# Two reorderings in a fused graph kernel: where the vector engine masks the moved score words, and how the first aggregation group is cut into pieces

## The chip, the cores and the metric

The kernel runs on one core of a Trainium2 chip. The metric is the device time of one execution in microseconds (us). The engines are named as the profile names them: PE (TensorE), DVE (VectorE), ACT (ScalarE), POOL (GpSimd) and SP (SyncE, which here only issues DMAs).

## What is computed

4096 nodes with 128 features, and a dense 4096 x 4096 adjacency of zeros and ones. Two layers, each behind a layer norm and a relu:

```python
h = jnp.maximum(_layernorm(x, axis=-1), 0.0)
# layer 0: attention over the edges
norm2 = jnp.linalg.norm(h, axis=1, keepdims=True)
cos = beta[0] * (h @ h.T) / (norm2 @ norm2.T + 1e-07)
P = jax.nn.softmax(cos + (1.0 - adj) * -1000000000.0, axis=1)
x = x + P @ h
h = jnp.maximum(_layernorm(x, axis=-1), 0.0)
# layer 1: mean over the neighbours
deg = jnp.clip(jnp.sum(adj, axis=1, keepdims=True), 1.0)
x = x + h @ W_self + (adj @ h / deg) @ W_neigh
```

## The kernel before

The attention is cut into 72 steps, k = 0 to 71. Step k handles a pair of 128-row tiles against a group of 512 rows: `PAIR[k] = (s, p, both)`. Cosines are symmetric, so one block of scores serves the pair twice where `both` holds: once as it is (the near side) and once turned (the far side).

For each step, in two halves of 512 columns (c = 0 and 1):

- PE multiplies the scores, six products for the two halves (L1058), into a ring of three PSUM banks. `ring_free` makes each item of the ring wait until the item three places earlier has been read out for the last time; for a score half that is its `low_part`.
- ACT takes the exponential twice, once as fp16 into `word` (L600) and once in fp32 in place (L601).
- DVE subtracts the two for the fp16 remainder, `low_part(k, c)` (L834). Both halves of a number then lie in one 32-bit word of `word`.
- POOL multiplies the words by the adjacency, `mask_near(k)` (L453), and PE multiplies the result with the table of features, `attend_near(k)` (24 matmuls, L1164, L1166, L1167).
- For most far sides PE turns the words (L1069) and DVE masks them, `mask_far` (L845). For 13 steps, the `MOVED` ones, the words are turned otherwise: DVE transposes blocks of 32 (`transpose_blocks`, L855), SP stores them to memory and fetches them back in another order into `moved_words`, and about four steps later DVE masks them, `mask_moved` (L866). The step in which PE uses them is their host, and `GUEST[k + 1]` is the moved step whose host is k + 1. PE uses the far words in `attend_far` (24 matmuls, L1139, L1141, L1142). The far sums lie in one bank, and DVE adds them to the rows with `spill` (L881, L886) before PE may start the next far pair.

PE's order in step k: the scores of step k + 2, `attend_far` of the far pair of this step if it has one, some transposes and products of the second layer, the turns for the next step, `attend_near(k)`. DVE's order in its step k is written out in `attention`: `low_part(k + 2, 0)`, `spill`, `mask_far(k + 1)`, `low_part(k + 2, 1)` and around these the rest. `mask_moved(GUEST[k + 1])` stands in DVE's step k; PE uses its result in its step k + 1, right behind the scores of k + 3. All engines work in the order of their code. Adjacency tiles come by DMA: the near ones issued by POOL (`load_near`, L445), the far ones by SP into the two buffers of `stage`, and POOL (L472) or ACT (L575) converts these into one byte each.

The names `item_next` and `RING[AT["score", k + 2, 1] + 1][0]` of the change ask what stands in the ring behind the second score half of step k + 2: the next score, or a transpose (`unit`, `h2`) or a `product` of the second layer.

Behind the attention PE aggregates (L1184): 8 groups of 512 rows, 128 matmuls each. Its first group is taken in pieces, `first_group(tiles, a, b)`, as filling between the last items of the second layer's features (`h2_transposes`, L1093; `h2_products`, L1108 to L1110). These items form the list `LATE` and alternate between two banks. Between them ACT makes the relu rows (`second_h`, L608), rounds the transposes (`h2_high`, L614), and DVE takes the rest (`h2_low`, L901).

Of the kernel before, what the change touches and what calls it, by code (L numbers as in the profile page):

```python
# [5 lines left out]
def gnn_program(nc, x_in, adj_in, beta_in, w_self_in, w_neigh_in, out):  # L6
# [12 lines left out]
    NP = len(PAIR)  # L19
# [7 lines left out]
    GUEST = {HOST[k]: k for k in MOVED}  # L27
    FAR_AT = [GUEST.get(k, k if k in NORMAL else None) for k in range(NP)]
# [3 lines left out]
    RING = [("score", 0, 0), ("score", 0, 1), ("score", 1, 0), ("score", 1, 1)]  # L32
# [13 lines left out]
    AT = {item: i for i, item in enumerate(RING)}  # L46
# [24 lines left out]
    with ctx:  # L71
# [108 lines left out]
        def far_adj(k, flat):  # L180

            s, p, _ = PAIR[k]
            g = p * 2 // TPS
            at = (g * T + s * TPS) * ROWS
            block = flat[:, at:at + TPS * ROWS].rearrange("p (t c) -> p t c", c=ROWS)
            return block[:, :, (p * 2 % TPS) * P:(p * 2 % TPS + 2) * P]
# [65 lines left out]
        def ring(buffer, k, c=0, chunks=2):  # L252

            at = k % 2 * TILE + c * ROWS
            return buffer[:, at:at + chunks * ROWS]
# [9 lines left out]
        def far_sem(m):  # L265
            return s_adjt_a if m % 2 else s_adjt_p
# [407 lines left out]
        def _(dve):  # L674
# [54 lines left out]
            def unit_low(g):  # L729

                dve.wait_ge(s_uhi, g + 1)
                dve.tensor_tensor(unit_lo(g * TPS, TPS), ps[:, transpose_bank(g), :], unit_hi(g * TPS, TPS), ALU.subtract
                                  ).then_inc(s_ulo, 1)
# [68 lines left out]
            def row_stats(s):  # L802

                dve.wait_ge(s_evac, 2 * (s + 1))
                for t in range(TPS):
                    done = step_of(dve.bn_stats(stats2[:, 6 * t:6 * (t + 1)], x_row(s * TPS + t)))
                return done

            def row_moments(s, done):

                dve.wait_ge(s_step, done)
                if s >= 2:
                    dve.wait_ge(s_rs2, s - 1)
                for t in range(TPS):
                    dve.bn_aggr(mv2(s)[:, t, :], stats2[:, 6 * t:6 * (t + 1)]).then_inc(s_var2, 1)

            def scale_scores(k, c):

                p, f = PAIR[k][1], ring(word, k, c, 1)
                at = 3 * (2 * k + c)  # L820
                dve.wait_ge(s_inv, 32 * (k + 1))
                dve.wait_ge(s_scores, 2 * k + c + 1)
                dve.tensor_scalar(f, f, inv_eps[:, 2 * p + c:2 * p + c + 1], 1.0, ALU.mult, ALU.add).then_inc(s_factor, 1)
                dve.wait_ge(s_factor, at + 1)
                dve.tensor_scalar(f, f, FACTOR_MAX, None, ALU.min).then_inc(s_factor, 1)
                dve.wait_ge(s_factor, at + 2)
                dve.reciprocal(f, f).then_inc(s_factor, 1)
                dve.wait_ge(s_factor, at + 3)
                dve.tensor_tensor(score(k, c), score(k, c), f, ALU.mult).then_inc(s_scaled, 1)

            def low_part(k, c):

                dve.wait_ge(s_exp, 2 * k + c + 1)
                dve.tensor_tensor(half(word16, k, c, 0, LOW, TPS), score(k, c), half(word16, k, c, 0, HIGH, TPS), ALU.subtract  # L834
                                  ).then_inc(s_elo, 1)

            def mask_far(k):

                m, n = FAR_BEFORE[k], N_BEFORE[k]
                dve.wait_ge(s_turn, n + 1)  # L840
                dve.wait_ge(far_sem(m), m // 2 + 1)
                at = ORDER.index(k)
                if at >= 2:
                    dve.wait_ge(s_pvt, at - 1)
                dve.tensor_tensor(  # L845
                    ring(far, at).rearrange("p (c t n) -> p c t n", c=2, t=TPS),
                    ps[:, TURN:TURN + 2, :].rearrange("p c (t n) -> p c t n", t=TPS),
                    far_adj(k, adj_t).rearrange("p t (c n) -> p c t n", c=2), ALU.mult).then_inc(s_far, 1)
# [9 lines left out]
            def mask_moved(k):  # L858

                m, i = FAR_BEFORE[k], M_BEFORE[k]  # L860
                dve.wait_ge(s_moved, 64 * (i + 1))
                dve.wait_ge(far_sem(m), m // 2 + 1)
                at = ORDER.index(k)
                if at >= 2:
                    dve.wait_ge(s_pvt, at - 1)
                dve.tensor_tensor(  # L866
                    ring(far, at).rearrange("p (c t q r) -> p c t q r", c=2, t=TPS, q=4),
                    slot[:, :].rearrange("p (q c t r) -> p c t q r", q=4, c=2, t=TPS),
                    far_adj(k, adj_t).rearrange("p t (c q r) -> p c t q r", c=2, q=4), ALU.mult).then_inc(s_far_m, 1)
# [43 lines left out]
            def attention(general):  # L913

                for k in range(2):
                    if general:
                        scale_scores(k, 0)
                        scale_scores(k, 1)
                    low_part(k, 0)
                    low_part(k, 1)  # L920
                    unit_low(k + 1)
                    if k == 0:
                        dve.wait_ge(s_hsum, 1)
                        dve.tensor_scalar(no_edge[:, 0:D], ps[:, 1, 0:D], TINY, None, ALU.mult).then_inc(s_mean, 1)
                for k in range(NP):
                    s, at = PAIR[k][0], k - FIRST[PAIR[k][0]]
                    if s >= 1 and at == 0:
                        new_rows(s - 1)
                    if s >= 1 and at == 1:
                        done = row_stats(s - 1)  # L930
                        if s == NS - 1:
                            row_moments(s - 1, done)
                    if s >= 1 and at == 2:
                        row_moments(s - 1, done)
                    if k + 1 in GUEST and FAR_AT[k] is None:
                        mask_moved(GUEST[k + 1])
                    if k + 2 < NP:
                        if general:
                            scale_scores(k + 2, 0)
                            scale_scores(k + 2, 1)  # L940
                        low_part(k + 2, 0)
                    if FAR_AT[k] is not None:
                        spill(FAR_AT[k])
                    if k + 1 in NORMAL:
                        mask_far(k + 1)
                    if k + 2 < NP:
                        low_part(k + 2, 1)
                    if k + 1 in GUEST and FAR_AT[k] is not None:
                        mask_moved(GUEST[k + 1])
                    if k % 2 == 0 and 3 <= k // 2 + 2 < NS:  # L950
                        unit_low(k // 2 + 2)
                    if k == 11:
                        split = weights_high()
                    if k == 13:
                        weights_low(split)
                    for g in range(EARLY):
                        after = k - (FIRST[g + 1] + 8)
                        if after == 0:
                            h2_low(g)
                        if after in (1, 2):  # L960
                            second_rows(g, after - 1)
                    if k + 2 in MOVED:
                        transpose_blocks(k + 2)
                new_rows(NS - 1)
                done = row_stats(NS - 1)
                row_moments(NS - 1, done)
                h2_low(5)
                second_rows(5, 0)
                second_rows(5, 1)
                h2_low(6)  # L970
                h2_low(7)
                second_rows(6, 0)
                second_rows(6, 1)
                second_rows(7, 0)
                second_rows(7, 1)
# [42 lines left out]
        def _(pe):  # L1018
# [160 lines left out]
            ALL = range(TPS)  # L1179
# [7 lines left out]
            def first_group(tiles, a, b):  # L1187

                pe.wait_ge(s_tab2, b // 2)
                for chunk in range(a, b):  # L1190
                    for t in tiles:
                        last = aggregate(0, t, chunk)
                return last
# [52 lines left out]
            pe.wait_ge(s_evac, 2 * (NS - 1))  # L1246
            first_group([0, 1], 0, 16)
            h2_transposes(5)
            first_group([3], 0, 8)
            h2_products(5, 0)  # L1250
            h2_products(5, 1)
            first_group([3], 8, 16)
            h2_transposes(6)
            first_group(ALL, 16, 20)
            h2_transposes(7)
            h2_products(6, 0)
            first_group(ALL, 20, 22)
# [89 lines left out]
```

## Time and profile before

| | |
|---|---|
| median of 3 runs | 485.01 us (484.8 to 486.03) |
| the profiled execution, its own time | 484.94 us |
| its span in the profile | 483.1 us |
| PE busy | 455.3 us, 94% |
| DVE, ACT, POOL busy | 294.9, 288.7, 264.0 us |
| granted TensorE clock | 1.0 (2.4 GHz) throughout |

The span lies 1.8 us under the profiled execution's own time. A matmul's end is modelled in the profile, so a block of matmuls is best read by the starts of its first and of the next block's first matmul.

### The profile page before, as it was taken

What the parts mean: (1) busy time and instruction counts of PE and PEld (TensorE: products, weight loads), DVE (VectorE), ACT (ScalarE), POOL (GpSimd) and SP (SyncE); (2) the same over time, 40 slices, a digit from 0 to 9 for tenths busy, and PEclk for the clock granted to TensorE, in tenths of its full rate; (3) what the DMA queues carried; (4) which work ended last, traced back from release to release, by engine and by line L of the source; (5) the groups of instructions that cost most, each with busy time, mean ns of one, the idle gap of its engine ahead of it and who ended that gap; (6) DMA issues with size and microseconds to landing.
All of it is one profiled execution on the core that took longest, in us unless ns stands there. A gap on an engine that the chain in (4) does not pass through costs nothing.

```text
span 483.1 us, 12207 instructions
## 1 busy us (share of the span) xinstructions
PE 455.3 (94%) x5096; PEld 380.3 (79%) x5096; DVE 294.9 (61%) x685; ACT 288.7 (60%) x437; POOL 264.0 (55%) x249
## 2 busy tenths in 40 slices
PE   0969999999999999999999998999999999999997
PEld 0837888788788887788777877887797888888886
DVE  6966656877676776768857777685776421022232
ACT  2999898767977768976797778677864000000000
POOL 3989777867958578775787578566562000000000
PEclk9999999999999999999999999999999999999999
DMA  8157879878799788997799598846500000000000
GB/s 245 28 65 153 173 141 215 196 167 163 158 232 211 156 194 148 239 208 162 137 216 222 87 203 199 188 69 98 79 3 2 6 23 20 23 23 23 23 23 22
DMA packets 45899, 59.68 MB, mean 124 GB/s; under 512 B 3600, under 2 KB 38672, under 8 KB 45840
## 3 DMA queue, kind: packets, MB, share of 16 engines
q1 hardware_dynamic: 35472, 49.42, 33.2%
q0 software_dynamic: 10368, 9.44, 24.6%
q8 instruction: 40, 0.66, 0.6%
q14 instruction: 19, 0.16, 0.1%
HBM read 78.25 MB, written 8.91 MB: 180 GB/s over the span
## 4 chain that ended last, share of the span: by engine, by line
PE 72%; ACT 12%; DVE 9%; issue 3%; POOL 2%; DMA 1%; SPq 0%; ACTq 0%; DVEq 0%; POOLq 0%
PE ps L1184 22%; PE ps L1058 13%; PE ps L1069 7%; ACT word L600 6%; PE ps L1167 5%; PE ps L1164 5%; PE ps L1166 5%; PE ps L1139 5%; PE ps L1142 4%; ACT ps L601 4%; PE ps L1141 4%; DVE far L866 3%; DVE word L834 1%; DVE adj_t L689 1%; DMA x_sb<-in_x_dram 1%
## 5 line engine op out<-in xcount | busy, mean ns | idle before, releaser
L453 POOL TENSOR_TENSOR near<-word,adj_t 128x1024 f32<-128x1024 f32 x72 | 151.8, 2108 | 82.9 <-DVE word L834 66.5
L600 ACT ACTIVATE word<-ps,small 128x512 f16<-128x512 f32 x144 | 136.2, 946 | 63.9 <-PE ps L1058 63.5
L834 DVE TENSOR_TENSOR word<-ps,word 128x512 f16<-128x512 f32 x144 | 105.9, 738 | 81.9 <-ACT ps L601 81.7
L1184 PE MATMUL ps<-table,adj_t 128*128 128x257 f16 x1024 | 115.0, 274 | 0.0
L1058 PE MATMUL ps<-unit_t 128*128 128x512 f16 x432 | 106.5, 379 | 6.7 <-DVE word L834 4.8
L1184 PEld LDWEIGHTS ps<-table,adj_t 128*128 128x128 fp8e4 x1024 | 100.0, 98 | 13.6
L601 ACT ACTIVATE ps<-ps,small 128x512 f32<-128x512 f32 x144 | 108.2, 751 | 0.0
L1164 PE MATMUL ps<-table,near 128*128 128x129 f16 x576 | 102.6, 219 | 2.2 <-POOL near L453 1.5
L1167 PE MATMUL ps<-table,near 128*128 128x129 f16 x576 | 102.9, 222 | 0.0
L1166 PE MATMUL ps<-table,near 128*128 128x128 f16 x576 | 102.6, 219 | 0.0
L1139 PE MATMUL ps<-table,far 128*128 128x129 f16 x448 | 80.0, 219 | 2.5 <-DVE far L866 2.0
L1142 PE MATMUL ps<-table,far 128*128 128x129 f16 x448 | 80.0, 222 | 0.0
L1141 PE MATMUL ps<-table,far 128*128 128x128 f16 x448 | 79.8, 219 | 0.0
L1058 PEld LDWEIGHTS ps<-unit_t 128*128 128x128 f16 x432 | 38.8, 98 | 43.3 <-DVE word L834 10.7
L1164 PEld LDWEIGHTS ps<-table,near 128*128 128x128 f16 x576 | 57.0, 99 | 5.0 <-POOL near L453 1.3
L845 DVE TENSOR_TENSOR far<-ps,adj_t 128x1024 f32<-128x1024 f32 x43 | 52.5, 1222 | 10.9 <-PE ps L1069 10.8
L1166 PEld LDWEIGHTS ps<-table,near 128*128 128x128 f16 x576 | 55.9, 97 | 1.6
L1167 PEld LDWEIGHTS ps<-table,near 128*128 128x128 f16 x576 | 56.2, 98 | 0.0
L1139 PEld LDWEIGHTS ps<-table,far 128*128 128x128 f16 x448 | 44.3, 99 | 14.6 <-DVE far L866 6.1
L1141 PEld LDWEIGHTS ps<-table,far 128*128 128x128 f16 x448 | 43.5, 97 | 4.8
L1069 PE MATMUL ps<-ident,word 128*128 128x128 f32 x344 | 44.7, 273 | 0.0
L1142 PEld LDWEIGHTS ps<-table,far 128*128 128x128 f16 x448 | 43.8, 98 | 0.0
(88 smaller groups left out, 472.7 us busy)
## 6 DMA issues: line engine op xcount, KB each, us to landing
stage<-in_adj_dram SPq DMA_DIRECT2D x56, 512.0 KB, 5.4
adj_t<-in_adj_dram POOLq DMA_DIRECT2D x72, 128.0 KB, 5.0
turned_blocks<-packed SPq DMA_DIRECT2D x13, 512.0 KB, 4.4
moved_words<-turned_blocks SPq DMA_DIRECT2D x52, 128.0 KB, 4.5
x_sb<-in_x_dram SPq DMA_DIRECT2D x4, 512.0 KB, 6.3
x_again<-in_x_dram SPq DMA_DIRECT2D x7, 256.0 KB, 5.8
out_dram<-x_sb SPq DMA_DIRECT2D x7, 256.0 KB, 2.3
far<-in_x_dram SPq DMA_DIRECT2D x1, 256.0 KB, 5.1
```

The source lines that it names most:

```text
L453: pool.tensor_tensor(ring(near, k), ring(word, k), adj_t[:, near_adj(k)], ALU.mult).then_inc(s_near, 1)
L600: act.activation(half(word16, k, c, 0, HIGH, TPS), score(k, c), ACT.Exp, bias=exp_bias, scale=exp_scale)
L601: act.activation(score(k, c), score(k, c), ACT.Exp, bias=exp_bias, scale=exp_scale).then_inc(s_exp, 1)
L834: dve.tensor_tensor(half(word16, k, c, 0, LOW, TPS), score(k, c), half(word16, k, c, 0, HIGH, TPS), ALU.subtract).then_inc(s_elo, 1)
L1058: ins = pe.matmul(score(k, c), j, rows, start=i == 0, stop=i == 2)
L1139: pe.matmul(far_acc(c), high, tab(rows, D, TW), start=c == 0 and t == 0, stop=False, skip_group_check=True)
L1141: pe.matmul(far_acc(c, 0, D), high, tab(rows, 0, D), start=False, stop=False, skip_group_check=True)
L1142: last = pe.matmul(far_acc(c), low, tab(rows, D, TW), start=False, stop=t == TPS - 1, skip_group_check=True)
L1164: pe.matmul(acc(s, t), high, tab(rows, D, TW), start=first and c == 0 and t % 2 == 0, stop=False, skip_group_check=True)
L1166: pe.matmul(acc(s, t, 0, D), high, tab(rows, 0, D), start=False, stop=False, skip_group_check=True)
L1167: last = pe.matmul(acc(s, t), low, tab(rows, D, TW), start=False, stop=end and c == 1, skip_group_check=True)
L1184: return pe.matmul(ps[:, agg_bank(g, t), 0:TW], adj_t[:, at:at + P], tab(b), start=(b == 0), stop=(b == T - 1))
```

## The change

DVE's `mask_moved` had two places: ahead of `low_part(k + 2, 0)` in steps whose own far pair is missing, and otherwise behind `low_part(k + 2, 1)`. Now it stands between the two low halves, behind `spill`, unless the ring has a transpose or product behind the second score half of step k + 2; then it stands behind `low_part(k + 2, 1)`, as before. Of the 13 masks six go from behind the second low half to ahead of it (DVE steps 11, 15, 19, 28, 36, 48), three go from ahead of the first low half to behind it (32, 44, 56), and four stay (24, 40, 52, 61). In the late part of PE, eight aggregation matmuls go from behind the products of group 5 to ahead of them, and eight from behind the transposes of group 6 to ahead of those.

```diff
-                    if k + 1 in GUEST and FAR_AT[k] is None:
-                        mask_moved(GUEST[k + 1])
                     if k + 2 < NP:
...
                         low_part(k + 2, 0)
                     if FAR_AT[k] is not None:
                         spill(FAR_AT[k])
                     if k + 1 in NORMAL:
                         mask_far(k + 1)
+                    item_next = k + 3 < NP and RING[AT["score", k + 2, 1] + 1][0] != "score"
+                    if k + 1 in GUEST and not item_next:
+                        mask_moved(GUEST[k + 1])
                     if k + 2 < NP:
                         low_part(k + 2, 1)
-                    if k + 1 in GUEST and FAR_AT[k] is not None:
+                    if k + 1 in GUEST and item_next:
                         mask_moved(GUEST[k + 1])
...
             h2_transposes(5)
-            first_group([3], 0, 8)
+            first_group([3], 0, 16)
             h2_products(5, 0)
             h2_products(5, 1)
-            first_group([3], 8, 16)
+            first_group(ALL, 16, 18)
             h2_transposes(6)
-            first_group(ALL, 16, 20)
+            first_group(ALL, 18, 20)
             h2_transposes(7)
             h2_products(6, 0)
```

On DVE, at the first of the six places (step 11), the order before: L881 is `spill`, the L834 behind it `low_part(13, 1)`, L866 the mask of the words of step 8.

```order
L855 STREAM_TRANSPOSE packed<-word 128x1024
L834 TENSOR_TENSOR word<-ps,word 128x512
L881 TENSOR_TENSOR x_sb<-ps,no_edge 128x2x129
L834 TENSOR_TENSOR word<-ps,word 128x512
L866 TENSOR_TENSOR far<-moved_words,adj_t 128x1024
L891 TENSOR_SCALAR w_parts<-adj_t 128x256
```

And now:

```order
L855 STREAM_TRANSPOSE packed<-word 128x1024
L834 TENSOR_TENSOR word<-ps,word 128x512
L881 TENSOR_TENSOR x_sb<-ps,no_edge 128x2x129
L866 TENSOR_TENSOR far<-moved_words,adj_t 128x1024
L834 TENSOR_TENSOR word<-ps,word 128x512
L891 TENSOR_SCALAR w_parts<-adj_t 128x256
```

The mask and the second low half have changed places.

On DVE, at the first of the three places (step 32), the order before: the mask of the words of step 29 stands between the row moments (L815) and both low halves of step 34.

```order
L834 TENSOR_TENSOR word<-ps,word 128x512
L855 STREAM_TRANSPOSE packed<-word 128x1024
L815 BN_AGGR small<-small 128x2 x4
L866 TENSOR_TENSOR far<-moved_words,adj_t 128x1024
L834 TENSOR_TENSOR word<-ps,word 128x512 x3
L886 TENSOR_TENSOR x_sb<-ps,x_sb 128x2x129
```

And now:

```order
L834 TENSOR_TENSOR word<-ps,word 128x512
L855 STREAM_TRANSPOSE packed<-word 128x1024
L815 BN_AGGR small<-small 128x2 x4
L834 TENSOR_TENSOR word<-ps,word 128x512
L866 TENSOR_TENSOR far<-moved_words,adj_t 128x1024
L834 TENSOR_TENSOR word<-ps,word 128x512 x2
L886 TENSOR_TENSOR x_sb<-ps,x_sb 128x2x129
```

The first low half of step 34 has gone ahead of the mask; the second still follows it.

On PE, behind the last attention step, the order before (L1184 the aggregation, L1093 the transposes of groups 5, 6 and 7, L1108 to L1110 the products of group 5, four times, and then of group 6):

```order
L1184 MATMUL ps<-table,adj_t 128x257 x32
L1093 MATMUL ps<-ident,unit_t 128x128 x4
L1184 MATMUL ps<-table,adj_t 128x257 x8
L1108 MATMUL ps<-w_parts,unit_t 128x256
...
L1184 MATMUL ps<-table,adj_t 128x257 x8
L1093 MATMUL ps<-ident,unit_t 128x128 x4
L1184 MATMUL ps<-table,adj_t 128x257 x16
L1093 MATMUL ps<-ident,unit_t 128x128 x4
L1108 MATMUL ps<-w_parts,unit_t 128x256
```

And now (each line number is one higher):

```order
L1185 MATMUL ps<-table,adj_t 128x257 x32
L1094 MATMUL ps<-ident,unit_t 128x128 x4
L1185 MATMUL ps<-table,adj_t 128x257 x16
L1109 MATMUL ps<-w_parts,unit_t 128x256
...
L1185 MATMUL ps<-table,adj_t 128x257 x8
L1094 MATMUL ps<-ident,unit_t 128x128 x4
L1185 MATMUL ps<-table,adj_t 128x257 x8
L1094 MATMUL ps<-ident,unit_t 128x128 x4
L1109 MATMUL ps<-w_parts,unit_t 128x256
```

Sixteen instead of eight matmuls stand between the transposes and the products of group 5, and eight instead of sixteen between the transposes of group 6 and of group 7.

## Rows read from the trace of the kernel before

**Rows 1.** Page, busy time and share of PE

```profile
PE 455.3 (94%) x5096; PEld 380.3 (79%) x5096; DVE 294.9 (61%) x685; ACT 288.7 (60%) x437; POOL 264.0 (55%) x249
```

**Rows 2.** Waits of PE: waiting line, releaser, us in total, times, longest

```profile
PE ps L1058 <- DVE word L834: 4.8, 5, 1.9
PE ps L1139 <- DVE far L866: 2.0, 6, 0.4
```

**Rows 3.** Timelines of DVE, POOL, PE, DVE's step 11: start, us, engine, line, operation

```profile
87.42 0.41 DVE L881 TENSOR_TENSOR x_sb<-ps,no_edge 128x258 f32<-128x258 f32 x1
88.24 0.73 DVE L834 TENSOR_TENSOR word<-ps,word 128x512 f16<-128x512 f32 x1 [0.41 <-ACT ps L601]
88.87 1.21 DVE L866 TENSOR_TENSOR far<-moved_words,adj_t 128x1024 f32<-128x1024 f32 x1
...
87.65 1.06 POOL L472 TENSOR_SCALAR adj_t<-stage 128x1024 uint8<-128x1024 f32 x1
...
88.45 1.46 PE L1058 MATMUL ps<-unit_t 128*128 128x512 f16 x6
90.13 0.23 PE L1139 MATMUL ps<-table,far 128*128 128x129 f16 x1 [0.22 <-DVE far L866]
```

**Rows 4.** Timeline of PE at DVE's step 48

```profile
258.59 1.46 PE L1058 MATMUL ps<-unit_t 128*128 128x512 f16 x6
260.41 0.23 PE L1139 MATMUL ps<-table,far 128*128 128x129 f16 x1 [0.36 <-DVE far L866]
```

**Rows 5.** Timelines of POOL and PE at DVE's step 19

```profile
122.85 2.02 POOL L453 TENSOR_TENSOR near<-word,adj_t 128x1024 f32<-128x1024 f32 x1 [0.20 <-DVE word L834]
125.52 2.12 POOL L472 TENSOR_SCALAR adj_t<-stage 128x1024 uint8<-128x1024 f32 x1
...
124.95 1.46 PE L1058 MATMUL ps<-unit_t 128*128 128x512 f16 x6
```

**Rows 6.** Timelines of ACT, DVE and PE at DVE's step 32

```profile
184.01 0.73 ACT L601 ACTIVATE ps<-ps,small 128x512 f32<-128x512 f32 x1
...
184.38 1.73 DVE L866 TENSOR_TENSOR far<-moved_words,adj_t 128x1024 f32<-128x1024 f32 x1
...
184.97 0.81 PE L1058 MATMUL ps<-unit_t 128*128 128x512 f16 x3
186.80 0.82 PE L1058 MATMUL ps<-unit_t 128*128 128x512 f16 x3 [1.02 <-DVE word L834]
187.46 0.22 PE L1139 MATMUL ps<-table,far 128*128 128x129 f16 x1
```

**Rows 7.** Timelines of POOL, DVE and PE at DVE's step 56

```profile
293.99 2.01 POOL L453 TENSOR_TENSOR near<-word,adj_t 128x1024 f32<-128x1024 f32 x1
...
294.28 2.79 DVE L866 TENSOR_TENSOR far<-moved_words,adj_t 128x1024 f32<-128x1024 f32 x1
...
298.43 0.22 PE L1139 MATMUL ps<-table,far 128*128 128x129 f16 x1
```

**Rows 8.** Converts that wait for a DMA, on POOL and ACT

```profile
144.81 1.04 POOL L472 TENSOR_SCALAR adj_t<-stage 128x1024 uint8<-128x1024 f32 x1 [3.43 <-DMA stage<-in_adj_dram]
...
194.32 1.06 ACT L575 ACTIVATE adj_t<-stage 128x1024 uint8<-128x1024 f32 x1 [0.19 <-DMA stage<-in_adj_dram]
```

**Rows 9.** Windows: stretch, its us, busy by engine, PEclk, DMA share, GB/s

```profile
128.00:145.00 17.00, 17.00 (x211) 14.18 (x209) 11.02 (x15) 14.14 (x22) 11.11 (x10) 1.00 0.98 231
```

**Rows 10.** Timelines of PE and DVE behind the attention

```profile
367.55 0.27 PE L1108 MATMUL ps<-w_parts,unit_t 128*128 128x256 f16 x1 [1.04 <-DVE unit_t L901]
368.86 1.06 PE L1184 MATMUL ps<-table,adj_t 128*128 128x257 f16 x8
369.76 0.60 PE L1093 MATMUL ps<-ident,unit_t 128*128 128x128 f32 x4
372.40 0.27 PE L1108 MATMUL ps<-w_parts,unit_t 128*128 128x256 f16 x1
...
371.49 0.69 DVE L901 TENSOR_TENSOR unit_t<-ps,unit_t 128x512 f16<-128x512 f32 x1 [1.25 <-ACT unit_t L614]
```

## The prediction

> **What bounds the kernel now.** I read the page first: PE is busy for 455.3 us [rows 1], and no other engine comes near that. So time can be won only where PE stands still. The waits of PE are the second view. Apart from its start, the largest are two kinds: score products wait for a low half of DVE, 4.8 us in five cases, and far attention waits for the mask of the moved words, 2.0 us in six [rows 2]. The first sum has three cases in which the low half is late because a mask stands ahead of it. The idle time of this view understates a delay, since a matmul's modelled end lies behind the moment at which the next may start; so the delays are taken from starts in the timeline. Three score products last 0.66 us until the next block (186.80 to 187.46) [rows 6], six last 1.30.
>
> **The six masks moved ahead of the second low half.** At step 11 [rows 3] the scores begin at 88.45, so the far attention could start at 89.75. It starts at 90.13, 0.05 behind the end of the mask (88.87 + 1.21 = 90.08): 0.38 us late. DVE took the spill at 87.42 to 87.83, stood still for 0.41 because the second exponential was not there, took the low half, and only then the mask. The change puts the mask into that idle time: it could run from 87.8 to 89.0. Against it speaks POOL: its convert runs from 87.65 to 88.71. Step 19 [rows 5] shows that the two engines can hold each other up: the same convert lasts 2.12 us there instead of 1.06, under a mask. Step 56 [rows 7] shows the other direction: the mask begins at 294.28, POOL's near mask runs until 296.00, and the mask ends at 297.07, which is 1.07 behind it; it needs only 1.21 alone. A mask held by a convert stands in no row. If it is not held, the whole 0.38 is won; if it is, it ends at 88.71 + 1.07 = 89.78, far attention starts at 89.83 and 0.30 is won. I take 0.30, since the near mask, the nearest row, does hold it.
>
> The Trainium skill, page SBUF — State Buffer, section Who interferes with whom, says that a DVE instruction with two SBUF inputs contends with a GpSimd instruction that reads SBUF, and that whichever issues first keeps the shared pair for its whole length. By that rule the convert holds the mask and the sum loses 0.08 us here; without it the sum would be 0.08 us better. Rows 5 and 7 agree with it in their two directions.
>
> At step 48, the last of the six, far attention could start at 258.59 + 1.30 = 259.89 and starts at 260.41: 0.52 late [rows 4]. The four between are late by 0.49 to 0.54. Of these step 19 has a hold: the near mask ends at 124.87 [rows 5], so the moved mask ends at 125.94 instead of some 124.4 + 1.2 = 125.6. PE can start at 124.95 + 1.30 = 126.25, so the hold costs nothing. At the other places POOL is between two operations or issues a DMA when the mask can start. I count 2.05 for the four. Sum of the six: 0.30 + 2.05 + 0.52 = 2.87 us.
>
> What is late instead is the second low half, by 0.6 to 0.8 us (the mask of 1.21 less the idle 0.41; at step 11 with the hold 1.5) [rows 3]. Behind it wait the near mask of step k + 2, used by PE only at the end of its step k + 2, two steps of some 5 us later; a turn one step later; and a ring item of step k + 4, or of k + 3 where another item follows, and exactly there the mask stays behind. A low half itself lasts 0.73 [rows 3]. In exchange the near mask is no longer held by the moved one. So I cost the delay at nothing; if it were not covered, each place would pay up to 0.8.
>
> **The three masks moved behind the first low half.** At step 32 [rows 6] the second exponential of the first half ends at 184.74, but DVE has begun the mask at 184.38, which lasts until 186.11 (held by the near mask that began before it). The low half comes behind it, PE's fourth score product only at 186.80, and far attention at 187.46. Now the low half goes from 184.8 to 185.5 and the score products go on without a wait: they would be through at 184.97 + 1.30 = 186.27. The mask goes from 185.4 to 186.6, since POOL's near mask is past, and far attention starts at about 186.68. That wins 0.78 of the 1.19. At step 44 the same rows recur; I take 0.79. At step 56 [rows 7] the near mask holds the moved mask in either place: it ends at 297.07 as before, but the low half now lies ahead of it. Far attention starts at 297.12 instead of 298.43: 1.31 us. Sum of the three: 2.88 us.
>
> **The pieces of the first group.** PE waits for the rest of the group-5 transposes before their products, which start at 367.55 after 1.04 us of idle time [rows 10]. Eight more matmuls ahead of them take 0.90 us (368.86 to 369.76) and fit into that wait, so the products start where they did. The next eight take the same time as those that stood there. But between the transposes of group 6 and the products of group 6 eight matmuls are now missing, and these products need DVE's L901, which ends at 372.18 [rows 10], and which hangs on ACT's chain, not on PE. They start at 372.40 now, with almost no room. They would be ready for 371.5, and must wait until about 372.33. So nearly all of the 0.90 is given back one item later: I count 0.07. Bounds: 0 and, if that chain were faster than in the rows, 0.90.
>
> **What DMA gives back.** The masks' 1.3 us from steps 11 to 19 move PE and the exponentials forward, not a transfer that is already waited for. In the stretch from 128 to 145 us the DMA engines are busy for 0.98 of the time [rows 9], and a convert at 144.81 has waited 3.43 us for its tile [rows 8]; behind it in POOL's queue stands a near mask, which holds the moved mask of step 24. The load was issued behind SP's store of transposed blocks. At step 19 these blocks are transposed behind mask and low half: at 125.94 + 0.63 = 126.57, before at about 126.74. So the load shifts by 0.17 at this step where PE shifts by 0.54: 0.4 us is given back at step 24. Bounds: 0 and all 1.3. The second such place is the ACT convert at 194.32, which waits 0.19 [rows 8]. Its load was issued before the 0.78 of step 32 is won. Bounds 0 and 0.78; I take the middle, 0.4, since the delay passes through two engines with some room before PE sees it.
>
> **Sum.** 2.87 + 2.88 + 0.07 - 0.4 - 0.4 = 5.0 us. The profiled execution took 484.94 us (span 483.1 and 1.8 around it), 0.07 under the median of the runs, which I take as the same. Forecast: 479.9 us, 1.0% faster.
>
> **The rivals.**
> - All is kept. DMA starts earlier as the whole of the pass does, and nothing is given back at 144.8 and 194.3: 484.94 - 5.82 = 479.1. For it: few converts wait for a load at all. Against it: the two rows that do [rows 8].
> - DMA takes back what it can, 1.3 at 144.8 and 0.78 at 194.3: 484.94 - 5.82 + 2.08 = 481.2. For it the DMA share of 0.98 [rows 9]; against it that loads follow buffers that come free earlier too.
> - The late second low half is waited for, at half of the places in which it is later, with 0.8 us each: 5.0 - 3 x 0.8 = 2.6 us won, 482.3. Against it the two steps until it is used.
> - Slower: POOL's near mask holds the moved mask in its new place. Where the whole near mask of 2.01 [rows 7] ran into it, the mask of step 48 would end near 258.1 + 2.0 + 1.07 = 261.2 and far attention be 0.8 us later than now, instead of 0.52 earlier. It decides against the change from the point at which the near mask of the step before ends later than 259.3 there (260.36 less 1.07). At all six places that is 6 x 0.8 = 4.8 us lost, with 2.88 won at the other three and 0.07: 486.6. Against it: of the places worked out, only at step 19 is a near mask in the way, and there the moved mask still ends 0.3 before PE needs it.
>
> **Chances and range.** The forecast, 479.3 to 480.6: 0.50. All kept: 0.20. DMA takes back: 0.20. The low half waited for: 0.07. Held by POOL: 0.03. A measurement of this kernel can tell about 0.3% (1.45 us) from no change. Faster than 483.5 are the first three cases and most of the fourth: 0.94; within it 0.03; slower 0.03. The range from 478.6 to 482.3 leaves out about 0.1, and it reaches from a full gain with a mask that no convert holds and 0.3 of the pieces, to the third rival.
>
> **What the profile would show.** Far attention at the nine hosts starts 1.30 behind its scores, except about 0.1 late at step 11 and 0.4 at steps 32 and 44 and 0.75 at step 56. The wait of score products for the low half falls from 4.8 us to about 1. The two converts wait longer, and step 24 is later by 0.4. The products of group 5 wait 0.2, those of group 6 about 0.6. Near masks last 2.0 instead of 2.9 where the moved mask held them. I would be wrong if the near attention of PE began to wait for POOL, or if the converts' waits grew by the whole gain.

## The result, and the profile after

| | before | changed | ratio, 95% interval |
|---|---|---|---|
| median of 6 runs each | 484.9 us (484.62 to 486.22) | 479.8 us (478.86 to 480.96) | 0.9888 [0.9871, 0.9906] |
| profiled execution | 484.94 us, span 483.1 | 480.36 us, span 478.6 | 4.58 us less |

The changed kernel is 1.1% faster. The forecast was 479.9 us. The page of the changed kernel:

```profile
span 478.6 us, 12207 instructions
PE 454.5 (95%) x5096; PEld 379.8 (79%) x5096; DVE 291.9 (61%) x685; ACT 288.3 (60%) x437; POOL 259.9 (54%) x249
```

PE works as long as before [rows 1]; what went away is standing still. POOL is busy for 4.1 us less; its near masks alone fell by 4.5 us (the mean of 72 from 2108 to 2046 ns), since fewer are held by a moved mask. The waits of PE after, in the columns of [rows 2] (each line number is one higher):

```profile
PE ps L1140 <- DVE far L866: 1.7, 4, 0.6
...
PE ps L1165 <- POOL near L453: 1.5, 2, 0.8
PE ps L1059 <- DVE word L834: 1.1, 3, 0.7
...
PE ps L1140 <- DVE far L845: 0.7, 2, 0.4
PE ps L1109 <- DVE unit_t L901: 0.6, 1, 0.6
```

The wait for the low half went from 4.8 to 1.1 us; what is left stands at 28, 39 and 75 us, ahead of the first moved mask. The wait for the moved mask shows 1.7 instead of 2.0, though it is now later at step 24 and at steps 32, 44 and 56 the delay was booked to the low half before. The table below tells these apart. The near attention waits as it did in the trace of before (1.5 us, twice), and no wait for a low half is left behind 75 us, so the later second low half cost nothing.

Measured as start of the far attention less start of its scores less 1.30, the lateness in us at DVE's steps with a moved mask is:

| step | 11 | 15 | 19 | 24 | 28 | 32 | 36 | 44 | 48 | 56 |
|---|---|---|---|---|---|---|---|---|---|---|
| before | 0.38 | 0.49 | 0.54 | 0.20 | 0.52 | 1.19 | 0.49 | 1.18 | 0.52 | 2.06 |
| after | 0.09 | 0 | 0 | 0.80 | 0 | 0.40 | 0 | 0.39 | 0 | 0.77 |

(At 40, 52 and 61 it is 0 in both. At step 44 after, part of the score block has no records; the 0.39 is read in the profiles of x_later, x_later_pieces and only32_44_56 below, and the idle time ahead of the far attention, 0.24 us, is the same as at step 32.) Without step 24 these nine places win 5.72 us; the prediction had 5.75. The timelines of DVE, POOL and PE at step 11, in the columns of [rows 3]:

```profile
87.77 2.03 DVE L866 TENSOR_TENSOR far<-moved_words,adj_t 128x1024 f32<-128x1024 f32 x1
89.72 0.73 DVE L834 TENSOR_TENSOR word<-ps,word 128x512 f16<-128x512 f32 x1
...
87.66 1.06 POOL L472 TENSOR_SCALAR adj_t<-stage 128x1024 uint8<-128x1024 f32 x1
...
88.46 1.46 PE L1059 MATMUL ps<-unit_t 128*128 128x512 f16 x6
89.85 0.23 PE L1140 MATMUL ps<-table,far 128*128 128x129 f16 x1
```

The mask sits in DVE's old idle time, but POOL's convert began 0.11 us earlier and holds it: it takes 2.03 and ends at 89.80, which is 1.08 behind the end of the convert (88.72). That was the direction for which the trace of before had no row. The rule of the Trainium skill (page SBUF — State Buffer, section Who interferes with whom) that whichever issues first keeps the shared pair holds in this row too. At step 32, to be read against [rows 6]:

```profile
184.18 0.74 DVE L834 TENSOR_TENSOR word<-ps,word 128x512 f16<-128x512 f32 x1 [0.30 <-ACT ps L601]
184.81 1.21 DVE L866 TENSOR_TENSOR far<-moved_words,adj_t 128x1024 f32<-128x1024 f32 x1
...
184.38 1.46 PE L1059 MATMUL ps<-unit_t 128*128 128x512 f16 x6
186.08 0.23 PE L1140 MATMUL ps<-table,far 128*128 128x129 f16 x1 [0.24 <-DVE far L866]
```

The low half waits for ACT, goes first, and six score products run in one block; the mask is no longer held (1.21 instead of 1.73). At step 56 [rows 7] it is still held, by a near mask from 290.79 to 292.80, but now as the only thing ahead of PE:

```profile
290.79 2.01 POOL L453 TENSOR_TENSOR near<-word,adj_t 128x1024 f32<-128x1024 f32 x1
...
292.31 1.57 DVE L866 TENSOR_TENSOR far<-moved_words,adj_t 128x1024 f32<-128x1024 f32 x1
...
291.87 1.46 PE L1059 MATMUL ps<-unit_t 128*128 128x512 f16 x6
293.94 0.23 PE L1140 MATMUL ps<-table,far 128*128 128x129 f16 x1 [0.61 <-DVE far L866]
```

What was given back lies between 128 and 149 us. First ACT's convert in the trace of before, then ACT, DVE, POOL and PE in the changed kernel, then the window of [rows 9]:

```profile
138.43 1.06 ACT L575 ACTIVATE adj_t<-stage 128x1024 uint8<-128x1024 f32 x1 [1.31 <-DMA stage<-in_adj_dram]
```

```profile
138.86 1.06 ACT L575 ACTIVATE adj_t<-stage 128x1024 uint8<-128x1024 f32 x1 [2.55 <-DMA stage<-in_adj_dram]
...
142.33 1.21 DVE L845 TENSOR_TENSOR far<-ps,adj_t 128x1024 f32<-128x1024 f32 x1
...
146.96 1.91 DVE L866 TENSOR_TENSOR far<-moved_words,adj_t 128x1024 f32<-128x1024 f32 x1
...
144.75 1.04 POOL L472 TENSOR_SCALAR adj_t<-stage 128x1024 uint8<-128x1024 f32 x1 [4.38 <-DMA stage<-in_adj_dram]
145.76 2.02 POOL L453 TENSOR_TENSOR near<-word,adj_t 128x1024 f32<-128x1024 f32 x1
...
143.60 0.23 PE L1140 MATMUL ps<-table,far 128*128 128x129 f16 x1 [0.41 <-DVE far L845]
...
148.92 0.23 PE L1140 MATMUL ps<-table,far 128*128 128x129 f16 x1 [0.65 <-DVE far L866]
...
128.00:145.00 17.00, 16.59 (x200) 13.34 (x197) 9.66 (x14) 14.45 (x23) 9.62 (x10) 1.00 0.99 225
```

ACT's convert waits 2.55 us instead of 1.31 and starts 0.43 later than before. The convert on POOL starts at 144.75, 0.06 earlier than before, and its wait has grown from 3.43 to 4.38 us [rows 8]. The near mask behind it ends at 147.78, and the moved mask, held by it, at 148.87; so the landing of the tile sets when the far attention of step 24's mask can start. It starts at 148.92; before it was 148.97. So the three early masks, worth 1.32 us until then, have won 0.05 by this point in this execution: 0.08 was given back at the far attention of 133.16 (1.38 behind its scores instead of 1.29), 0.57 at 143.60 and 0.60 at 148.92. From there to the far attention of step 61 (323.29 before, 318.81 now) PE gains another 4.43; the six late places of the table add up to 4.40. With the pieces' 0.09 that is, but for rounding, the 4.58 between the profiled executions. Behind the attention, PE and then DVE:

```profile
360.98 1.96 PE L1185 MATMUL ps<-table,adj_t 128*128 128x257 f16 x16
363.08 0.27 PE L1109 MATMUL ps<-w_parts,unit_t 128*128 128x256 f16 x1
...
366.61 0.61 PE L1094 MATMUL ps<-ident,unit_t 128*128 128x128 f32 x4
367.86 0.27 PE L1109 MATMUL ps<-w_parts,unit_t 128*128 128x256 f16 x1 [0.64 <-DVE unit_t L901]
...
367.02 0.69 DVE L901 TENSOR_TENSOR unit_t<-ps,unit_t 128x512 f16<-128x512 f32 x1 [1.25 <-ACT unit_t L614]
```

By starts, the wait ahead of the products of group 5 went from 1.20 to 0.31 us; a new one of 0.80 stands ahead of the products of group 6.

### The profile page after: what moved, and what is told of

Same layout as the page of the kernel before. It is cut to its first block, busy times and chain, and to the rows that moved or that the text cites. A ratio compares the mean times of both kernels' runs of the same rounds, so it can differ in the third digit from the quotient of the medians.

```text
span 478.6 us, 12207 instructions
## 1 busy us (share of the span) xinstructions
PE 454.5 (95%) x5096; PEld 379.8 (79%) x5096; DVE 291.9 (61%) x685; ACT 288.3 (60%) x437; POOL 259.9 (54%) x249
## 4 chain that ended last, share of the span: by engine, by line
PE 77%; DVE 8%; ACT 8%; issue 2%; POOL 2%; DMA 1%; SPq 0%; ACTq 0%; DVEq 0%; POOLq 0%
PE ps L1185 22%; PE ps L1059 15%; PE ps L1070 7%; PE ps L1168 6%; PE ps L1165 5%; PE ps L1167 5%; PE ps L1140 5%; PE ps L1143 5%; PE ps L1142 5%; ACT word L600 3%; ACT ps L601 2%; DVE far L866 1%; DVE far L845 1%; DVE word L834 1%; DVE adj_t L689 1%
## 5 line engine op out<-in xcount | busy, mean ns | idle before, releaser
L453 POOL TENSOR_TENSOR near<-word,adj_t 128x1024 f32<-128x1024 f32 x72 | 147.3, 2046 | 82.0 <-DVE word L834 65.6
L834 DVE TENSOR_TENSOR word<-ps,word 128x512 f16<-128x512 f32 x144 | 106.2, 737 | 82.6 <-ACT ps L601 82.2
```

The lines of the kernel that those rows point to most:

```text
L453: pool.tensor_tensor(ring(near, k), ring(word, k), adj_t[:, near_adj(k)], ALU.mult).then_inc(s_near, 1)
```

## The experiments

The kernel before ran again beside each of three groups of kernels, and each ratio is to the runs of its own group. The groups are masks_only, pieces_only, early3 and late6 (median of the kernel before 485.53 us); only19, only11_15, x_later and pieces_later (484.91 us); and the rest (484.9 us).

### The masks alone, the pieces alone

masks_only is the changed kernel with the pieces as before:

```diff
             h2_transposes(5)
-            first_group([3], 0, 16)
+            first_group([3], 0, 8)
...
-            first_group(ALL, 16, 18)
+            first_group([3], 8, 16)
             h2_transposes(6)
-            first_group(ALL, 18, 20)
+            first_group(ALL, 16, 20)
```

> Only the masks are moved; the pieces of the first group stand as before. Theory: the masks carry nearly all of the gain, 4.5 us in the profiled execution (5.7 us won at the nine places, 1.25 given back between 128 and 149 us), and the products of group 5 wait 1.2 us again: 480.4 us or up to 0.7 below it. Rival: the pieces carry a good part of the gain (up to 0.9 us, the eight matmuls that now lie in the wait): then this one is 0.9 us slower than the changed kernel.

pieces_only is the kernel before with this diff the other way round.

> Only the pieces of the first group are placed anew; the masks stand as before. Theory: 0.1 us faster than before, since the wait of 1.2 us ahead of the products of group 5 falls to 0.3 and 0.8 us of waiting appears ahead of the products of group 6. Rival: the wait goes away for good and 0.9 us are won.

Measured: masks_only 480.12 us, 0.9885 [0.987, 0.99]; pieces_only 485.37 us, 0.9998 [0.9989, 1.0007]. masks_only came out as its theory said. The masks are the whole win that can be measured; the pieces do nothing that the times can show, and their profile has waits of 0.30 and 0.80 us in place of one of 1.20. It also holds a row of another kind, at step 19 (POOL, DVE, PE):

```profile
125.50 1.04 POOL L472 TENSOR_SCALAR adj_t<-stage 128x1024 uint8<-128x1024 f32 x1
...
125.58 2.04 DVE L866 TENSOR_TENSOR far<-moved_words,adj_t 128x1024 f32<-128x1024 f32 x1
...
127.67 0.23 PE L1139 MATMUL ps<-table,far 128*128 128x129 f16 x1 [1.28 <-DVE far L866]
```

In the trace of [rows 5] the mask and the convert both start at 125.52, and the convert was held; here, with the same code at this place, the convert came first by 0.08 us and held the mask, and the far attention is 1.44 late instead of 0.54. I took from it a new theory: in the old order this race makes executions differ by some 0.9 us, and the new place of step 19 removes it.

### The early three, the late six

Built on masks_only, with the old places kept where the new name is false:

```diff
+                    moved_here = k < 24
+                    if k + 1 in GUEST and FAR_AT[k] is None and not moved_here:
+                        mask_moved(GUEST[k + 1])
...
-                    if k + 1 in GUEST and not item_next:
+                    if k + 1 in GUEST and not item_next and moved_here:
...
-                    if k + 1 in GUEST and item_next:
+                    if k + 1 in GUEST and (item_next or not moved_here and FAR_AT[k] is not None):
```

> Of the masks only those of steps 11, 15 and 19 are moved; pieces as before. Theory of the pinned loads: the loads of adjacency tiles between 128 and 147 us land when they land, whatever PE wins before (138.4, 144.7 and 146.9 us), so the 1.3 us won at the three places are given back at step 24: 0 to 0.2 us faster than before, far attention of step 24 starts at 148.9 as before. Rival, the loss at step 24 is the hold between the moved mask and the near mask and does not hang on what was won earlier: 1.3 us faster.

For late6 only the first of these lines differs:

```diff
+                    moved_here = k > 24
```

> Of the masks only those of steps 28, 32, 36, 44, 48 and 56 are moved; pieces as before. Theory of the pinned loads: 4.4 us faster than before, as much as all nine together, since nothing behind 149 us waits for a load for more than 0.2 us. Rival, every place keeps what it wins: the same 4.4 us here, but then the nine together are faster by another 1.3 us than this one.

Measured beside the two above: early3 484.13 us, 0.9975 [0.9965, 0.9986], about 1.2 us; late6 481.1 us, 0.9917 [0.9904, 0.9931], about 4.0 us. The late six carry most of the win. For the early three the two kinds of evidence differ. The timed runs leave 1.2 us of 1.3, and masks_only is 1.0 us below late6: in both the rival's number came and not that of the theory. The profiled executions leave next to nothing: far attention of step 24's mask starts at 148.74 in early3, 148.65 in late6, where the early masks stand as before, and 149.16 in masks_only. A part of the difference may lie in which execution was profiled: in masks_only it was the slowest of four (480.78 us), in early3 the ninth of ten (484.68), in late6 the fastest of five (480.62). The changed kernel's is the fifth of six.

### Step 19 alone, steps 11 and 15 alone

```diff
+                    moved_here = k == 19
```

> Of the masks only that of step 19 is moved; pieces as before. Theory of the race: before, DVE's moved mask and POOL's convert become ready 0.04 to 0.08 us apart at step 19, and where the convert is first the mask ends 0.9 us later; most executions of the kernel before are of that kind (485.5 us), a few of the other (484.8). The mask ahead of the second low half ends before the convert starts in either kind. So 485.5 falls by 0.9 + 0.54 = 1.4 us less what loads give back behind it, 0.2 to 0.6: 484.3 us median. Rival, no race, and the move is worth the 0.54 us of the profiled execution: 485.0 us median.

```diff
+                    moved_here = k < 16
```

> Of the masks only those of steps 11 and 15 are moved; pieces as before. Theory of the race: 0.8 us are won at the two places, all later work of PE, DVE and POOL up to step 19 moves as one, and the race at step 19 is as before; together with the loads between 128 and 147 us this leaves 0.3 to 0.8 us: 484.7 to 485.2 us. Rival, the early masks' whole gain of three (1.2 us) comes from these two: 484.3 us.

Measured: only19 485.07 us, 1.0 [0.9984, 1.0017]; only11_15 484.51 us, 0.9979 [0.996, 0.9999]. The theory of the race as the cause of the scatter fell: with the mask of step 19 in its new place the times still reach from 484.13 to 486.74. Its median came out at the rival's 485.0. That alone would say less, since the kernel before had a median of 484.91 beside it and not the 485.5 from which the theory had reckoned. only11_15 lies between its two forecasts and decides nothing. The profile of only19 shows the mask's far attention on time, and then POOL's convert:

```profile
144.90 1.04 POOL L472 TENSOR_SCALAR adj_t<-stage 128x1024 uint8<-128x1024 f32 x1 [3.83 <-DMA stage<-in_adj_dram]
```

It starts 0.09 later than in [rows 8], and the far attention of step 24's mask at 149.07, 0.73 late. The 0.5 us of step 19 went there in this execution.

### One load out of the busy stretch

If the DMA engines' share of 0.99 sets when the tiles of this stretch land, taking bytes out of it must bring them forward. The kernel reloads 256 KB of x for the second group (`load_x_again(1)`) in SP's step 24, in the middle of it; here that goes to step 29.

```diff
-                    if k == min(FIRST[again] + 8, NP - 1):
+                    if k == min(FIRST[again] + (13 if again == 1 else 8), NP - 1):
```

> The changed kernel with one load issued later: the 256 KB of rows that are read again for group 1 go from SP's step 24 (about 127.5 us, in the stretch in which the DMA engines are fully busy) to its step 29 (about 148 us). Theory, the transfers of this stretch give the gain of the early masks back in part of the executions: the loads of 129.3 and 134.9 us land 1 us or more earlier, far attention of steps 23 and 24 waits for less than 0.3 us together instead of 1.4, and the time is 0.5 to 1.2 us below the changed kernel's: 478.9 us. Rival, the loads are held by something else than this transfer (the order of SP's queue behind the stored blocks): 479.8 us, as the changed kernel.

Measured: 479.22 us (478.86 to 479.94), 0.9879 [0.9852, 0.9905], profiled execution 479.13. The two converts in its profile:

```profile
136.99 1.06 ACT L575 ACTIVATE adj_t<-stage 128x1024 uint8<-128x1024 f32 x1 [0.72 <-DMA stage<-in_adj_dram]
...
143.55 1.03 POOL L472 TENSOR_SCALAR adj_t<-stage 128x1024 uint8<-128x1024 f32 x1 [3.23 <-DMA stage<-in_adj_dram]
```

They start 1.87 and 1.20 us earlier than in the changed kernel's profile. SP issued their loads at 128.99 and 134.82 instead of 129.34 and 134.91, only 0.35 and 0.09 us earlier. So the place of the reload in SP's queue, the rival's cause, can account for 0.35 us at most. ACT's convert lies clear of all six profiles with the early masks moved and the reload in the stretch (138.86 to 139.81); POOL's hardly does (143.62 to 144.75), so the 1.20 can be a difference between executions. The far attention of step 24's mask starts at 147.72, 1.2 us ahead of the changed kernel's profile and 0.24 late, and the profiled execution is 1.23 us shorter than the 480.36 of the changed kernel. The ratio, though, can't be told from the changed kernel's (0.9888 in the first comparison), so the reload's place is shown to move this stretch, not to shorten a typical execution.

### The pieces one item later

The wait of 0.80 us ahead of the products of group 6 is there because eight matmuls had been taken from it. pieces_later puts the eight of tiles 20 and 21 ahead of it.

```diff
             h2_transposes(7)
-            h2_products(6, 0)
             first_group(ALL, 20, 22)
+            h2_products(6, 0)
             h2_products(6, 1)
```

> The changed kernel with the eight aggregation matmuls of tiles 20 and 21 placed ahead of the products of group 6 instead of behind their first half. Theory, the 0.8 us of waiting ahead of these products is where the pieces' gain went: the matmuls fill it, the first half starts where it does now, the second needs the rest of the transposes of group 7 about 0.15 us later than PE comes: 0.65 us below the changed kernel, 479.2 us. Rival, the chain through ACT and DVE behind these products becomes late by as much (products of group 7 wait): no change against the changed kernel.

Measured: 478.46 us (478.08 to 479.69), 0.986 [0.9834, 0.9886], beside x_later; the new wait is gone from its profile. Against the changed kernel's 0.9888 that is some 1.3 us, against its other ratio (below) 0.8; the intervals overlap, so by the times the size is rough. The profiles have it more closely. From the far attention of step 61 to the end of the span it is 159.8 and 159.7 us in the two profiles of the changed kernel and 159.7 in x_later, but 159.0 in pieces_later and in x_later_pieces: 0.7 to 0.8 us, where the theory had 0.65.

### Both, beside the changed kernel

The two diffs above together.

> The changed kernel with both: the load of rows for group 1 issued at SP's step 29, and the eight matmuls ahead of the products of group 6. Theory, the two losses lie apart (128 to 149 us, and behind 360 us) and add: 0.65 us from the pieces and 0.5 from the load, 478.6 us or less, 1.2 us below the changed kernel. Rival, they don't add, or the load's part was only scatter between executions: 479.1 us.

The changed kernel once more, beside it:

> The changed kernel once more, beside the next three: 479.8 us, and the kernels of this call are compared with it.

Measured: x_later_pieces 478.2 us (478.04 to 478.35), 0.9855 [0.984, 0.9871]; after_again 479.41 us (478.89 to 480.04), 0.9877 [0.9861, 0.9894]. This is the best version, 1.2 us under the changed kernel; the two intervals overlap, but each of its four runs is faster than each of the other's four. Its runs differ by 0.3 us, those of the changed kernel by 1.15. By the profiles the pieces are 0.7 to 0.8 us of this. What the reload adds to a typical execution was not measured beside pieces_later alone, which with 0.986 is nearly as good. The converts, the far attention and the window in its profile, and then PE's tail:

```profile
137.24 1.06 ACT L575 ACTIVATE adj_t<-stage 128x1024 uint8<-128x1024 f32 x1 [0.90 <-DMA stage<-in_adj_dram]
...
142.08 1.04 POOL L472 TENSOR_SCALAR adj_t<-stage 128x1024 uint8<-128x1024 f32 x1 [1.70 <-DMA stage<-in_adj_dram]
...
147.60 0.23 PE L1140 MATMUL ps<-table,far 128*128 128x129 f16 x1
...
128.00:145.00 17.00, 17.00 (x207) 14.00 (x205) 10.92 (x16) 14.57 (x23) 12.27 (x11) 1.00 1.01 222
...
365.28 0.61 PE L1094 MATMUL ps<-ident,unit_t 128*128 128x128 f32 x4
365.73 1.05 PE L1185 MATMUL ps<-table,adj_t 128*128 128x257 f16 x8
366.61 0.27 PE L1109 MATMUL ps<-w_parts,unit_t 128*128 128x256 f16 x1
```

The DMA engines are as busy in the window as before (1.01; 0.95 in x_later), so the stretch is still nearly full; but the reload is no longer among the transfers, and POOL's convert runs 2.67 us earlier. The reload alone made it 1.20 us (x_later) and the pieces alone 0.17 (pieces_later, 144.58), so this 2.67 can't be put down to the reload; executions differ here. PE's matmuls fill the place of the wait.

Across the kernels, the start of that far attention tells which edits reach it:

| kernel | early masks | reload | far attention, us |
|---|---|---|---|
| before | old | in the stretch | 148.97 |
| late6, only32_44_56 | old | in the stretch | 148.65, 148.71 |
| only19, only11_15 | in part new | in the stretch | 149.07, 149.14 |
| early3, masks_only | new | in the stretch | 148.74, 149.16 |
| changed, after_again, pieces_later | new | in the stretch | 148.92, 148.61, 148.75 |
| x_later, x_later_pieces | new | behind it | 147.72, 147.60 |

Old and new early masks can't be told apart by this column; the place of the reload can. (pieces_only, with the convert first at step 19, has 149.70; all_between, below, changes step 24 itself and has 149.31.)

### Without the exception for ring items

all_between puts all thirteen masks between the low halves.

```diff
-                    if k + 1 in GUEST and not item_next:
+                    if k + 1 in GUEST:
                         mask_moved(GUEST[k + 1])
                     if k + 2 < NP:
                         low_part(k + 2, 1)
-                    if k + 1 in GUEST and item_next:
-                        mask_moved(GUEST[k + 1])
```

> The changed kernel without its exception: the masks of steps 24, 40, 52 and 61 too stand between the two low halves. Theory, there the ring hands the bank of the second low half to the next step's second scores, and DVE's mask of 1.2 us delays them: PE's fourth score product of the next-but-one step waits, at step 24 longest since the near mask holds the moved mask; far attention had waited at none of 40, 52 and 61, so nothing is won: 0.5 to 2.5 us slower than the changed kernel. Rival, the low half has room there as well: no change.

Measured: 480.49 us, 0.9898 [0.9881, 0.9915], beside after_again's 479.41. Intervals overlap at their edges; the profiles say where the 1.1 us goes (DVE at step 24, then PE at steps 24 and 52):

```profile
146.76 1.20 DVE L866 TENSOR_TENSOR far<-moved_words,adj_t 128x1024 f32<-128x1024 f32 x1
147.89 0.71 DVE L834 TENSOR_TENSOR word<-ps,word 128x512 f16<-128x512 f32 x1
...
148.66 0.82 PE L1057 MATMUL ps<-unit_t 128*128 128x512 f16 x3 [0.62 <-DVE word L834]
279.06 0.82 PE L1057 MATMUL ps<-unit_t 128*128 128x512 f16 x3 [0.52 <-DVE word L834]
```

The late low half ends at 148.60 and the second three score products of the block start 0.06 behind it. Far attention is 0.78 and 0.69 us late by starts at two of the four places, steps 24 and 52; at steps 40 and 61 nothing waits. The profile of after_again has 0.09 and 0 there, which makes 1.4 us, and the profiled executions differ by as much (481.46 to 480.04); the profile of the first comparison has 0.80 at step 24, from the landing of the tile, and against an execution of that kind step 24 would cost nothing. So the rival of the awaited low half is real at two of the four places where the exception keeps it out, and at none of the nine places of the change.

### The three masks behind the first low half alone

```diff
+                    moved_here = k in (32, 44, 56)
```

> Of the masks only those that stood ahead of the first low half are moved (steps 32, 44, 56); pieces as before. Theory, each wait is replaced by the shorter one of the mask itself and nothing gives it back: 2.9 us faster than before, the wait of score products for a low half falls from 4.8 us to 0.9. Rival, part is taken back by the convert at 194 us, which waits for its load: 2.1 to 2.5 us.

Measured: 481.92 us, 0.9933 [0.9919, 0.9947], 3.0 us under the kernel before; the prediction had 2.88. The waits of PE in early3, where these three masks stand as before, and in this kernel:

```profile
PE ps L1062 <- DVE word L834: 5.0, 6, 1.9
```

```profile
PE ps L1143 <- DVE far L866: 3.2, 9, 0.6
...
PE ps L1062 <- DVE word L834: 0.9, 2, 0.7
```

The wait for the low half goes with these three masks alone.

## Why the prediction came out right, and where it did not

- **Six masks, 2.87 us.** In the profile they win 2.85 at their places (0.29, 0.49, 0.54, 0.52, 0.49, 0.52). The choice of 0.30 instead of 0.38 at step 11, with the convert holding the mask, was measured as 0.29.
- **Three masks, 2.88 us.** 0.79, 0.79 and 1.29 in the profile, 3.0 by only32_44_56. Both the sizes and the mechanism were right, which of the two waits is left included.
- **Pieces, 0.07 us.** 0.09 in the profile; pieces_only, with 0.9998 [0.9989, 1.0007], can't tell it from nothing. That the win would be given back one item later was right, and pieces_later got it back.
- **What DMA gives back, 0.4 + 0.4 us.** This term was mis-sized at both places. In the profiled execution it was 1.27 at the first place and 0 at the second: ACT's convert near 193.2 waited 0.19 as before and PE saw nothing of it. I had reckoned that the load shifts by 0.17 where PE shifts by 0.54, and that the other gains stay. The first half of this holds roughly: the transpose of the blocks starts at 125.85 instead of 126.64, 0.79 earlier, where PE's far attention is 1.32 earlier. But the landing did not follow the issue. Of the two loads, the one issued 1.05 us earlier than before landed 0.43 later, and the one issued 0.67 earlier landed 0.06 earlier. The bound of all 1.3 was the value of this profile; that of after_again, with far attention at 148.61, gives back 0.96.
- **The luck in the number.** The profiled execution, 480.36, missed the forecast by 0.46 us, because 0.8 was taken off where 1.27 was given back. The median of 479.8 is within 0.1 us of it, because a typical execution gives back less: without any giving back the sum is 5.8 us and with all of the 1.3 it is 4.5, and the medians of the three comparisons give 5.1 and 5.5 for the changed kernel and 5.4 for masks_only, so 0.3 to 0.7 is given back where 0.8 was taken off.
- **Why runs and profiles differ.** The fastest run of a kernel compared with the fastest run of the kernel before beside it is 5.76 and 5.72 us less for the changed kernel, 5.78 for masks_only and 1.34 for early3; the places add up to 5.81, 5.72 and 1.32. So the fastest executions seem to keep everything, as the first rival had it, and the giving back happens in the others. The profiled executions of the kernels with all early masks in their new places and the reload in the stretch are the slowest of their runs or next to them, so they show the side on which most is given back. These are single runs and single profiles: no profile of a fastest execution of these kernels exists, and why the tiles land late in some executions stays open.
- **Rivals.** The low half is not waited for at the nine places (1.1 us of wait against 4.8, all of it ahead of them), and at these places no near mask made far attention later than before. The full giving back (481.2, both places) was half right in the profile: the first place, not the second. The recorded time of the slower rival, 486.6, is a slip; its own terms give 484.94 + 4.8 - 2.88 - 0.07 = 486.8. Its place in the ranking does not change.

## What to carry to other kernels

An operation that waits for nothing itself belongs in the idle time ahead of one that does, but only if nothing needs that one soon. Here the exchange is free at the six places where the ring has a score behind it, and costs 0.7 to 0.8 us at two of four places where a transpose or product follows. Where the DMA engines are full for a stretch, a microsecond won ahead of it may, in a part of the executions, end in a longer wait at its end; look then for a transfer in it that nobody needs yet. One profile is one execution: see where its time lies among the runs before a difference between two profiles is called the effect of an edit. A wait that a filler is taken from comes back at the next item, so follow the chain one item further before counting it as a win.

## What the runs showed of the hardware that was not expected

- The hold between DVE and POOL works in each direction, and at step 19 less than 0.1 us turned it: where both started at 125.52 the convert took 2.12 us; where the convert started 0.08 us before the mask it took 1.04 and the mask 2.04. The held mask ended 1.08 us behind the end of what held it, a convert or a near mask (89.80 to 88.72, 293.88 to 292.80).
- In a stretch with the DMA engines 0.98 to 0.99 busy, the landing of two tiles did not follow their issue. In five profiles with all early masks moved and the reload in the stretch (changed, after_again, masks_only, early3, pieces_later) their loads were issued 1.05 to 1.14 and 0.41 to 1.18 us earlier than before; ACT's convert, which needs the first, starts 0.43 to 1.38 us later, and POOL's, which needs the second, 0.06 to 1.19 earlier. With 256 KB moved to a later step ACT's convert starts at 136.99 and 137.24 instead of 138.86 to 139.81, and the far attention of step 24's mask at 147.72 and 147.60 instead of 148.61 to 149.16.
